# Turning the expert results with a product against two stacked identities instead of a transpose and an add

## What is computed

```
flat = x.reshape(-1, C)                        # 8192 tokens, C = 64
probs = softmax(flat @ router_w.T)
topk_probs, topk_idx = top_k(probs, 2)
gates = topk_probs / (sum(topk_probs) + 1e-9)  # per token and chosen expert
h1 = einsum('nc,ehc->neh', flat, w1)           # H = 682 hidden units, 8 experts
h3 = einsum('nc,ehc->neh', flat, w3)
h  = silu(h1) * h3
y  = einsum('neh,ech->nec', h, w2)
out = einsum('ne,nec->nc', gates, y)
```

## Time and profile before

| | |
|---|---|
| median of 3 runs | 809.62 us (809.58 to 811.24) |
| span of the profiled execution | 809.8 us |
| TensorE matmul / weight load busy | 664.6 us (82%) / 502.3 us (62%) |
| VectorE busy | 462.7 us (57%) |
| ScalarE busy | 354.0 us (44%) |
| GpSimd busy | 370.7 us (46%) |
| mean granted TensorE clock | 0.816 of full speed |
| chain that ended last, by engine | PE 49%, POOL 23%, issue 17%, DVE 6%, DMA 3% |

### The profile page before, as it was taken

The page is one execution under the profiler, slowest core; times in us unless marked ns, Lnnn a source line. Parts: engine busy times, 40 slices in busy tenths (PEclk is TensorE's granted clock), DMA queues, the critical chain, the costliest instruction groups (busy, mean ns, idle before and its releaser), DMA issues.

```text
span 809.8 us, 13968 instructions
## 1 busy us (share of the span) xinstructions
PE 664.6 (82%) x4632; PEld 502.3 (62%) x4632; DVE 462.7 (57%) x1094; ACT 354.0 (44%) x693; POOL 370.7 (46%) x377
## 2 busy tenths in 40 slices
PE   2598989797989797886404999999999999999960
PEld 1476768586867576673303777777777777777740
DVE  2256677677777777633311565566655666555645
ACT  1142737373737373523202544555445554455520
POOL 2203241767676768726662233443334433344440
PEclk9665868677777878555556999999999999999985
DMA  2000000010101010101183455556555555555508
GB/s 82 2 14 1 14 0 15 16 51 17 50 18 37 18 37 17 47 7 40 36 194 96 136 168 158 155 157 164 175 169 160 155 160 161 174 167 167 171 9 311
DMA packets 46615, 75.47 MB, mean 93 GB/s; under 512 B 7488, under 2 KB 30048, under 8 KB 46544
## 3 DMA queue, kind: packets, MB, share of 16 engines
q1 hardware_dynamic: 34512, 57.12, 24.2%
q0 software_dynamic: 8640, 12.74, 4.8%
q10 hardware_dynamic: 3392, 4.73, 1.8%
HBM read 58.54 MB, written 16.47 MB: 93 GB/s over the span
## 4 chain that ended last, share of the span: by engine, by line
PE 49%; POOL 23%; issue 17%; DVE 6%; DMA 3%; ACT 1%; POOLq 0%; SPq 0%; ACTq 0%; DVEq 0%
PE bk L747 25%; POOL expert_rows L496 15%; PE bk L758 12%; PE bk L735 3%; POOL rr L451 3%; PE bk L765 2%; DMA srow<-expert_results 2%; POOL r L462 2%; PE bk L553 1%; POOL x2t L480 1%; POOL r L457 1%; PE bk L577 1%; PE bk L570 1%; PE bk L638 1%; DMA small<-in_smalls 1%
## 5 line engine op out<-in xcount | busy, mean ns | idle before, releaser
L1256 DVE TENSOR_TENSOR units<-bk,silu 128x512 f32<-128x512 f32 x213 | 147.4, 692 | 164.7 <-ACT silu L933 164.7
L518 POOL DMA_INDIRECT expert_results<-yout,xin x142 | 139.5, 983 | 217.2 <-DVE yout L1267 190.4
L747 PE MATMUL bk<-xs,wbuf 64*128 64x256 f32 x1704 | 204.4, 386 | 1.2 <-ACT xs L920 1.1
L747 PEld LDWEIGHTS bk<-xs,wbuf 64*128 64x128 f32 x1704 | 160.0, 188 | 44.3 <-issue 26.7
L933 ACT ACTIVATE silu<-bk 128x512 f32<-128x512 f32 x213 | 127.2, 597 | 86.1 <-PE bk L747 86.1
L496 POOL DMA_INDIRECT expert_rows<-srow,pos x128 | 131.3, 1026 | 44.2 <-issue 38.0
L758 PE MATMUL bk<-units,wbuf 128*64 128x256 f32 x852 | 107.6, 388 | 0.0
L758 PEld LDWEIGHTS bk<-units,wbuf 128*64 128x64 f32 x852 | 54.8, 136 | 32.4 <-issue 11.7
L925 ACT ACTIVATE ysb<-bk 128x256 f32<-128x256 f32 x71 | 27.3, 384 | 84.2 <-PE bk L758 84.2
L451 POOL TENSOR_TENSOR rr<-vare,c_mhalf 128x16 f32<-128x16 f32 x8 | 23.4, 2923 | 79.3 <-DVE vare L1036 79.3
L735 PE MATMUL bk<-const,xin 128*128 128x128 f32 x142 | 31.3, 302 | 29.2 <-DMA xin<-expert_rows 29.2
(11 more groups left out here) (184 smaller groups left out, 981.5 us busy)
## 6 DMA issues: line engine op xcount, KB each, us to landing
wbuf<-in_weights SPq DMA_DIRECT2D x71, 576.0 KB, 4.0
xin<-expert_rows SPq DMA_DIRECT2D x71, 130.0 KB, 2.3
expert_results<-yout,xin POOLq DMA_INDIRECT x142, 2.8
xg<-in_x SPq DMA_DIRECT2D x8, 256.0 KB, 2.8
expert_rows<-srow,pos POOLq DMA_INDIRECT x128, 2.4
srow<-expert_results SPq DMA_DIRECT2D x8, 256.0 KB, 5.6
srow<-expert_results ACTq DMA_DIRECT2D x8, 256.0 KB, 6.4
out<-hid ACTq DMA_DIRECT2D x8, 256.0 KB, 5.8
```

The costliest lines, as they stand in the source:

```text
L518: g.indirect_dma_start(results[:, :], bass.IndirectOffsetOnAxis(ap=xin[:, t % X_SLOTS, h, ROW - 1:ROW].bitcast(U32), axis=0), yout[:, t % ...
L747: last = mm(bank[:, ch * MT:(ch + 1) * MT], wbuf[part, t % W_SLOTS, at:at + P], xs[part, t % 2, :], start=True, stop=True)
L1256: tt(units[:, t % 2, q, :], h3_ps[q], silu[:, q, :], ALU.mult).then_inc(unit_ready, 1)
```

## The change

`turn_results` becomes an ordinary matmul: the stationary operand is still a block of 128 rows of `ysb`, and the moving operand is `fold`, 128 by 64, two identities of 64 one above the other, instead of the 128 by 128 identity in transpose mode. The product turns the block and adds its two halves in the same product. `gate_out` then has one operation, the product with the gate, which reads PSUM. The constants grow by 64 columns, and `ysum` with its semaphore goes. No other instruction changes its place on any engine.

```
-CONSTS = dict(..., pad=2 * ROW, q_one=1, k_one=1)
+CONSTS = dict(..., pad=2 * ROW, q_one=1, k_one=1, fold=C)
...
+        fold = const_of("fold")
...
-        ysum = sb("ysum", [P, 2, 2, C])
...
             def turn_results(t):
                 pe.wait_ge(ysb_ready, t + 1)
                 for h in range(2):
-                    last = turn(yt_banks[t % 2][:, MT + h * P:MT + (h + 1) * P], ysb[:, t % 2, h * P:(h + 1) * P], ident)
+                    last = mm(yt_banks[t % 2][:, MT + h * C:MT + (h + 1) * C], ysb[:, t % 2, h * P:(h + 1) * P], fold,
+                              start=True, stop=True)
                 last.then_inc(y_turned, 1)
...
             def gate_out(t):
                 dve.wait_ge(y_turned, t + 1)
-                halves = yt_banks[t % 2][:, MT:2 * MT].rearrange("p (h a c) -> p h a c", h=2, a=2)
-                v.tensor_copy(ysum[:, t % 2, :, :], halves[:, :, 0, :]).then_inc(ysum_ready, 1)
-                dve.wait_ge(ysum_ready, 2 * t + 1)
-                tt(ysum[:, t % 2, :, :], halves[:, :, 1, :], ysum[:, t % 2, :, :], ALU.add).then_inc(ysum_ready, 1)
-                dve.wait_ge(ysum_ready, 2 * t + 2)
+                summed = yt_banks[t % 2][:, MT:MT + 2 * C].rearrange("p (h c) -> p h c", h=2)
                 dve.wait_ge(xin_loaded[t % X_SLOTS], 16 * (t // X_SLOTS + 1))
                 wait(dve, y_scattered[t % X_SLOTS], 32 * (t // X_SLOTS))
-                tt(yout[:, t % X_SLOTS, :, :], ysum[:, t % 2, :, :],
+                tt(yout[:, t % X_SLOTS, :, :], summed,
                    wide(xin[:, t % X_SLOTS, :, 2 * C], C), ALU.mult).then_inc(yout_ready, 1)
...
+    t["fold"][:] = p % C == np.arange(C)[None, :]
```

More of the change, by code:

```diff
@@ L45 @@
               v_heads=2 * HEADS, region=NE * NJ, scan_keep=NE * (NJ + 1), k_rows=T // MT, tile_no=1, tile_at=1,
-              pad=2 * ROW, q_one=1, k_one=1)
+              pad=2 * ROW, q_one=1, k_one=1, fold=C)
 SMALLS = dict(bias2=1, g1=1, b1=1, g2=1, b2=1, fc1_bias0=2, proj=C + M + 2 * C, fc1=DFF, fc2=2 * C, fc2_bias=C,
@@ L347, in hybrid_block @@
         y_turned = sem("y_turned")
-        ysum_ready = sem("ysum_ready")
         yout_ready = sem("yout_ready")
```

## The result

The changed kernel takes 821.8 us, the median of 4 runs (819.98 to 823.57), against 809.6 us; the ratio is 1.014, with a 95% interval of 1.0116 to 1.0163. By the ratio it is slower by 11.3 us (9.4 to 13.2), and the forecast was 821.0. The profiled execution has a span of 818.6 us and a time of 820.37 us.

A forecast was written before the change was run, and what follows sets the result against it. The prediction took TensorE's row of products to bound the expert loop: 809.8 + 11.9 (products) - 0.65 (VectorE at the end) + 0.1 (constants) = 821.2 us, median 821.0; 8-in-10 range 817 to 824.5.

The forecast's parts named there:

- What bounds the kernel: Expert loop: TensorE's row of products is the path, so each of 68 tiles changes by turn_results' time; VectorE is hidden.
- The products: turn_results: two transposes become four records, the pair 0.56 us instead of 0.38, +11.9 us over 68 tiles.
- The row of equal shape: L688 and L689, two products of exactly the new shape in succession, took 0.56 us, taken for the new pair.
- built from parts: New pair: first record behind transposes 0.23 with its load hidden, then three steps of 0.11, giving 0.56 us.
- a guess from two rows: TensorE: loading 128 stationary columns seems to set the 0.11 us step, as 64 and 128 moving columns step alike.
- The one on the other side: Rival for turn_results: each fold product makes one record, the pair takes 0.33 us, 805.7 us in all; chance 5%.
- Columns as the limit: Rival for turn_results: columns bind, not loads; the pair takes 0.39 us, 809.7 us in all, no change; chance 9%.
- The dearer pair: Rival for turn_results: an ordinary column takes four times a turned one, 824.1 us, or 826.8 with exposed first load; 10% together.
- VectorE and the end: gate_out: copy and add go, hidden inside the loop; at its end the last scatters start earlier, -0.65 us.
- The constants: Ahead of all else: loading 64 more columns, 33 KB at 322 GB/s, adds 0.1 us.
- The sum: Whole kernel: 809.8 + 11.9 - 0.65 + 0.1 = 821.2 us for a profiled execution, 821.0 for the median.
- The claim that 0.2% can be told apart: Whole kernel: about 0.2%, 1.6 us, is what a measurement can tell from no change.

The follow-up runs named there:

- e1_ordinary128: Kernel before, with turn_results as ordinary products with the 128-column identity instead of transposes, VectorE keeping its three operations; 823.81 us in one execution.
- e3_eight_columns: Changed kernel with only 8 of the 64 columns of fold in each product, so the output is not the reference's; 819.9 us in one execution.
- e4_two_tiles: Changed kernel with each product of turn_results split into two of 64 stationary columns, the array shape of down; 811.31 us, ratio to the kernel before 0.9999.
- the control: The kernel before, unchanged, measured against itself as if it were another kernel; ratio 1.0006 (0.9989 to 1.0024).

## Why the prediction was right

**What bounds the kernel.** Right. The period followed the pair, 0.38 to 0.56 and 4.82 to 5.00, and followed it again to 5.44 with the pair doubled. The 41 us that VectorE lost are not to be seen in the loop.

**The products.** Right, with the step that carried it: the records were counted in the trace, not in the program, where the pair looks like two products before and after. The row of equal shape gave 0.56, and 0.56 was measured. The same 0.56 built from parts, 0.23 and three steps of 0.11, was luck. In the changed kernel the view from 613.28 on shows the last three of the four records:

```profile
613.05 0.50 PE L764 MATMUL bk<-const,ysb 128*128 128x64 f32 x3
```

So the first step is 0.06 (613.05 - 612.99), not 0.11, and the last record takes 0.28, not 0.23: two errors that cancel. The first step could have been read from L688, whose two records take 0.33 (0.33 - 0.27 = 0.06).

That the load of the stationary columns sets the step was a guess from two rows; `e1_ordinary128`, `e3_eight_columns` and `e4_two_tiles` now show it from three sides: four loads take 0.53 with 128, 64 or 8 columns moving, and half the columns loaded step in half the time. It holds up to 128 moving columns, but there the load need not be the only limit: in the kernel before, four transposes with 65 stationary columns and 128 moving ones, at clock 1.00, step by (0.60 - 0.27) / 3 = 0.11 too.

```profile
268.45 0.60 PE L563 MATMUL bk<-const,n 128*65 128x128 f32 x4
```

The page "FP8 and Floating Point Precision" of the Trainium skill, TensorE Precision Notes, counts passes, four for true FP32; with 8 columns for 64 they would be an eighth as long, and the pair went from 0.56 to 0.51, so here they were not the limit.

**The rivals.** The one on the other side, one record a product, fell by the 284 records. Columns as the limit fell by `e3_eight_columns`. The dearer pair fell too: 0.56 and not 0.60 or 0.64, its first load hidden under the turned rows (L764's loads start at 612.88, 0.11 ahead of its first product). A factor of four against a transpose was not there at equal columns either: four records and 0.61 against two and 0.38.

**VectorE and the end.** Right: 0.65 forecast, 0.66 measured from the operation to the scatter, with the last tile's `yout` (793.83) well ahead of its scatter (796.58 - 1.29 = 795.29).

**The constants.** The 0.1 us could not be told from the 4 us by which the loop's start varies.

**The sum.** The difference was right, 11.35 forecast against 11.3 by the ratio (12.2 between the medians); the base was not. A span was taken for the time of its execution. The profiled run after took 820.37 with a span of 818.6, 1.8 more (in every run that has both it is 1.7 to 2.1), so by this difference the execution before with its 809.8 took about 811.6 and was itself some 2 us above its median. Since only the difference was carried over to the median, this did not show. It shows in a comparison of the two profiled spans: they are only 8.8 apart, since the loop of the one after started 2.3 earlier (433.8 against 436.1). The lengths of the loop, from the first to the last start of `turn_rows`, compare better: 337.1 and 338.4 in the two executions before, 349.0 and 348.6 in the two after, which is 10.2 to 11.9 longer where 11.9 was forecast. The claim that 0.2% can be told apart was at its edge: the control's interval reaches 0.17% down and 0.18% up from its middle.

## What to carry to other kernels

Before work moves onto the engine that bounds a stage, count in the trace how many records such an operation makes and at what step they run, from a row of the same shape: here an ordinary float32 product was two records where a transpose was one, and half the columns gave back 0.05 of 0.61 us. Work taken from an engine with time to spare gains only what lies at the stage's end, here 0.65 us. If the product is wanted, give it the shape of array that its neighbour has: against the kernel before, neither that nor turning rows by two gained anything alone; together they gave 0.5%.

## What the runs showed of the hardware

A change of the array's shape costs about 0.1 us, as much as one record of a run: `down`'s first load waits until the record before it is nearly out (613.48 in the changed kernel, 0.07 ahead of the modelled end of L764 at 613.55), and with the shape kept, in `e4_two_tiles`, it follows at the step of the run, 0.28 after the first of four steps. The Trainium skill's page "TensorEngine Tiling (Array Packing)", Key Properties, says that a change of tiling mode drains TensorE; the trace agrees to within these 0.07 us. The price ahead of the fold in `e4_two_tiles` was 0.09 us (0.37 for 0.28).

The stages ahead of the loop do not run alike twice: in the 23 runs of the kernel before beside the control, times from 808.06 to 814.12 go with mean granted clocks of 0.822 to 0.813, and every run at 0.822 took under 810 us. In the pages of before and after the slices of those stages show a granted clock of 5 to 9 tenths, that is from the level of 1.2 GHz to near that of 2.4, and differ from kernel to kernel; in the loop the clock is 1.00. What decides which pattern a run gets was not looked into.
